# Cross-attention values carried through the output weights per head, in a transformer block with two mixture-of-experts layers

## The reference, cut to what matters

```
h1 = adaln(x);  x = mha(h1, h1, wq1, wk1, wv1, wo1) + x          # self-attention
h2 = adaln(x);  x = mha(h2, context, wq2, wk2, wv2, wo2) + x     # cross-attention
h3 = adaln(x);  x = (a * gelu(gate)) @ w2 + x                    # feed-forward

mha: q, k, v = (xq @ wq, ctx @ wk, ctx @ wv) split in 16 heads of 64
     attn = softmax(q @ k.T / sqrt(64))                          # per head, 128 x 77
     out  = concat_heads(attn @ v) @ wo + bo
```

## Time and profile before

| | |
|---|---|
| median of 3 executions | 931.8 us (930.72 to 932.12) |
| the profiled execution | 932.87 us, span 931.1 us, mean granted clock 0.917 |
| PE busy | 796.0 us, 85% |
| DVE, ACT, POOL busy | 568.6 us (61%), 540.7 us (58%), 360.9 us (39%) |
| hardware DMA queue of SP | 40027 packets, 70.09 MB, 23.5% of 16 engines |

### The profile page before, as it was taken

How to read it: one execution, slowest core, us unless ns; L and a number is a source line. 1 busy time by engine, 2 the same in 40 slices (tenths; PEclk the granted TensorE clock), 3 DMA queues, 4 the chain that set the end, 5 groups by cost and what they waited for, 6 DMA issues and landing times.

```text
span 931.1 us, 19002 instructions
## 1 busy us (share of the span) xinstructions
PE 796.0 (85%) x6173; PEld 666.3 (72%) x6173; DVE 568.6 (61%) x1941; ACT 540.7 (58%) x1147; POOL 360.9 (39%) x559
## 2 busy tenths in 40 slices
PE   5989999999999999999987688999977776861693
PEld 4767778878788888888866456999746565651693
DVE  1687778777776767766674352333458787885012
ACT  3656677666776667666764222333448898851462
POOL 1344344333433323233655150566413222226362
PEclk9999999999999999999998689999956979795797
DMA  9532033206030001000200131888500000001574
GB/s 280 198 129 107 1 129 129 106 2 231 5 120 34 19 2 37 16 23 16 65 12 19 46 105 47 241 252 246 201 18 1 1 0 1 1 1 38 164 204 125
DMA packets 43612, 78.50 MB, mean 84 GB/s; under 512 B 5564, under 2 KB 28812, under 8 KB 42876
## 3 DMA queue, kind: packets, MB, share of 16 engines
q1 hardware_dynamic: 40027, 70.09, 23.5%
q0 software_dynamic: 3488, 7.20, 2.2%
HBM read 63.98 MB, written 30.13 MB: 101 GB/s over the span
## 4 chain that ended last, share of the span: by engine, by line
PE 56%; DVE 21%; issue 8%; ACT 6%; POOL 6%; DMA 2%; DVEq 0%; SPq 0%; ACTq 0%; POOLq 0%
PE bank L635 6%; PE bank L909 5%; PE bank L697 5%; PE bank L660 4%; PE bank L650 3%; DVE sb_smax L1406 3%; PE bank L641 3%; PE bank L685 3%; PE bank L669 3%; PE bank L917 3%; DVE sb_row_sum L1416 3%; PE bank L1018 2%; DVE sb_st_all L1714 2%; PE bank L726 2%; PE bank L1026 2%
## 5 line engine op out<-in xcount | busy, mean ns | idle before, releaser
L1891 POOL TENSOR_TENSOR sb_expd<-sb_expd,sb_rden 128x512 f32<-128x512 f32 (+1 forms) x128 | 112.5, 880 | 248.3 <-DVE sb_rden L1420 248.2
L1406 DVE TENSOR_REDUCE sb_smax<-bank 128x4 f32<-128x512 f32 (+1 forms) x128 | 74.1, 579 | 59.1 <-PE bank L660 34.8
L1983 POOL TENSOR_TENSOR sb_rstd_all<-sb_rsq_all,sb_halves 128x4 f32<-128x4 f32 x44 | 45.2, 1028 | 130.7 <-DVE sb_rsq_all L1721 130.7
L685 PE MATMUL bank<-sb_eye,sb_expd 128*128 128x128 f32 (+1 forms) x512 | 77.7, 279 | 5.8 <-POOL sb_expd L1891 5.3
L1128 ACT ACTIVATE sb_expd<-sb_shifted 128x512 f32<-128x512 f32 (+1 forms) x128 | 69.8, 545 | 19.0 <-DVE sb_shifted L1409 18.0
L685 PEld LDWEIGHTS bank<-sb_eye,sb_expd 128*128 128x128 f32 (+1 forms) x512 | 60.0, 145 | 26.4 <-issue 13.2
L1122 ACT ACTIVATE sb_probT<-bank 128x512 f32<-128x512 f32 (+1 forms) x128 | 74.3, 590 | 7.2 <-PE bank L685 7.0
L1409 DVE TENSOR_TENSOR sb_shifted<-bank,sb_smax 128x512 f32<-128x512 f32 (+1 forms) x128 | 75.0, 586 | 4.4
L1416 DVE TENSOR_REDUCE sb_row_sum<-sb_expd 128x4 f32<-128x512 f32 (+1 forms) x128 | 73.0, 570 | 5.5 <-ACT sb_expd L1128 5.5
L635 PE MATMUL bank<-sb_h1T,sb_watt 128*128 128x128 f32 x512 | 71.6, 286 | 4.7 <-ACT sb_h1T L1045 2.3
L697 PE MATMUL bank<-sb_probT,sb_v 128*64 128x128 f32 (+1 forms) x1024 | 70.2, 279 | 5.0 <-issue 3.4
(11 more groups left out here) (256 smaller groups left out, 1905.7 us busy)
## 6 DMA issues: line engine op xcount, KB each, us to landing
sb_up_w<-gate_up SPq DMA_DIRECT2D x38, 384.0 KB, 4.1
rows_b<-pad_b SPq DMA_DIRECT2D x7, 1105.0 KB, 8.5
rows_a<-pad_a SPq DMA_DIRECT2D x7, 975.0 KB, 6.4
sb_up_w<-w1b SPq DMA_DIRECT2D x23, 256.0 KB, 3.5
sb_v<-v_all SPq DMA_DIRECT2D x16, 308.0 KB
v_all<-sb_v_rows SPq DMA_DIRECT2D x9, 512.0 KB, 2.6
sb_blk_x<-rows_a SPq DMA_DIRECT2D x38, 65.0 KB, 3.0
sb_watt<-att_w SPq DMA_DIRECT2D x4, 512.0 KB, 6.6
```

The costliest lines, as they stand in the source:

```text
L685: mm = pe.transpose(trans[u % 2][0:n, h, :], expd[:, (units_before(i) + u) % EXP_RING, h, 0:n], eye[:, :])
L1406: dve.tensor_reduce(smax[:, u % 2, :], s_in, X, ALU.max).then_inc(max_done, 1)
L1891: pool.tensor_tensor(e, e, rden[:, u % 2, :].unsqueeze(2).broadcast_to([P, QH, n]), ALU.mult).then_inc(norm_done, 1)
```

## The change

The cross values are now multiplied by the output weights before the attention. For each head `h`, `b2[h] = wv2[h] @ wo2[h]` is a 128 x 128 matrix; the four pieces `b2_0` to `b2_3` (four matmuls over 64 rows each) are made once, in iteration 0, and kept as 128 x 2048 in the place of the old weights. A block of values is then `context @ b2`, 2048 columns wide, in four pieces `v2_0` to `v2_3` (steps 6, 7, 9 and 10) where there were two (steps 0 and 4). `v2_all` has one row of 128 floats for each batch, head and key: 16 x 77 = 1232 rows per batch. The probabilities of a batch lie side by side as 128 x 1232 (`expd2`), are transposed in 10 chunks of 128 instead of 16 of 77 (2, 2, 3 and 3 in the four units), and the result is one accumulation of 10 matmuls at step 1 (`cross_out`, the new `wo2`). The 16 value matmuls per batch and the two `oTB` copies are gone.

`v2_rows` keeps its 128 x 1024, so it holds half a block. SP stores the first half when `v2_0` and `v2_1` are copied, the second when `v2_2` and `v2_3` are, each in one DMA for every batch that the block touches (`v2_pieces`). ACT waits with the copy of `v2_2` until the first half has landed. The load of a batch's values stands at the head of the next iteration, ahead of that iteration's stores, and needs `wo2` of two batches earlier to be over.

`v1_1` moves from step 7 to 11, `zT` from step 10 to 11, `logit` behind `v1_1`. DVE adds `wo2` to the residual ahead of the maximum of u2, where it stood behind the sum of u1. The Gelu is written over its input. The value weights' load of 512 KB moves behind that of x, transposed.

```diff
 FILL = [
-    (("h2T", "v2_0"), ("g2_5",)),
+    (("h2T",), ("g2_5",)),
     (("a2_0", "a2_1"), ("a2_2", "wo2", "rank")),
-    (("q1_1",), ("k1_0",)),
-    (("k1_1", "a2_3"), ("q1_0",)),
-    (("h3T", "v2_1"), ("g2_4",)),
-    (("g2_0", "g2_1", "g2_3"), ("gate",)),
-    (("lin",), ()),
-    (("v1_1",), ()),
+    (("q1_1", "b2_0"), ("k1_0",)),
+    (("k1_1", "a2_3"), ("q1_0", "b2_1")),
+    (("h3T", "b2_2"), ("g2_4",)),
+    (("g2_0", "g2_1", "g2_3"), ("gate", "b2_3")),
+    (("lin",), ("v2_0",)),
+    (("v2_1",), ()),
     (("wo1",), ("g2_2", "ffout")),
-    ((), ("hT",)),
-    ((), ("v1_0", "zT")),
-    (("logit",), ()),
+    (("v2_2",), ("hT",)),
+    ((), ("v1_0", "v2_3")),
+    (("zT", "v1_1"), ("logit",)),
 ]
+def v2_pieces(n):
+    found, last = [], min(P * (n + 1), B * C)
+    for b in range(P * n // C, -(-last // C)):
+        first, end = max(P * n, C * b), min(last, C * (b + 1))
+        found.append((b, first - C * b, end - C * b, first - P * n, end - P * n))
+    return found
...
             def store_values(i):
                 n = V2_BLOCK[i]
-                last = min(P, B * C - P * n)
-                sp.wait_ge(emptied["act"], max(PLAN[i, "v2_0"][2], PLAN[i, "v2_1"][2]))
-                sp.dma_start(v2_all[P * n:P * n + last, :], v2_rows[0:last, :]).then_inc(v2_stored, 16)
+                by_batch = v2_all.rearrange("(b h k) d -> b k h d", h=H, k=C)
+                for half in range(2):
+                    sp.wait_ge(emptied["act"], max(PLAN[i, f"v2_{2 * half + j}"][2] for j in range(2)))
+                    for b, k0, k1, p0, p1 in v2_pieces(n):
+                        sp.dma_start(by_batch[b, k0:k1, 8 * half:8 * half + 8, :],
+                                     v2_rows[p0:p1, :].rearrange("p (h d) -> p h d", h=8)).then_inc(v2_stored, 16)
...
             def values(i):
+                if i >= 1:
+                    load_values(i - 1)
                 if i in V2_BLOCK:
                     store_values(i)
-                load_values(i)
...
+            def cross_out(i, name):
+                t = use(i, name)
+                for c in range(CHUNKS):
+                    k = min(P, H * C - P * c)
+                    mm = pe.matmul(t[:, 0:D], probT2[0:k, c, :], v2[0:k, i % 2, c, :], start=(c == 0), stop=(c == CHUNKS - 1))
                 mm.then_inc(proj_full, 1)
...
-                    if n and name == last_of(i, "v2", first=True):
-                        act.wait_ge(v2_stored, 16 * n)
-                    empty(i, name, v2_rows[0:last, half * 512:(half + 1) * 512], lambda t: t[0:last, :])
+                    if name == "v2_0":
+                        from_one(act, v2_stored, 16 * v2_stores(n))
+                    if name == "v2_2":
+                        act.wait_ge(v2_stored, 16 * (v2_stores(n) + len(v2_pieces(n))))
+                    empty(i, name, v2_rows[0:last, half % 2 * 512:(half % 2 + 1) * 512], lambda t: t[0:last, :])
...
                 for k in range(N_STEPS):
+                    if k == AT["wo2"] and "C" in S:
+                        dve.wait_ge(xab_ready, c + 1)
+                        residual(i, "wo2", xb[:, :], tile(x0b, c))
                     if scored(k):
                         softmax_in(i, scored(k)[0], scored(k)[2])
                     if summed(k) and k != AT["sums"]:
-                        softmax_sums(i, summed(k)[0], summed(k)[2])
+                        softmax_sums(i, *summed(k))
                     if k == AT["wo2"] and "C" in S:
-                        dve.wait_ge(xab_ready, c + 1)
-                        residual(i, "wo2", xb[:, :], tile(x0b, c))
```

170 lines of the change are left out of this document (101 added, 69 removed).

## The result

The changed kernel takes 979.1 us (median of 4 runs, 977.66 to 982.12), the kernel before 931.6 in the same session: a ratio of 1.0515, 95% interval 1.0488 to 1.0541, so 47 us slower. The profiled execution is 979.36 us with a span of 977.6 and a mean granted clock of 0.895 (before 0.917).

What follows compares the result with a forecast made beforehand. PE and a chain over DVE and ACT were taken as level, within some tenths, from `gate` to `zT`. Work -5.5, wait +36 and clock +6 gave +36.5: 968 us on the median, range 945 to 984.

Steps and rivals of the forecast that it cites:

- Equal shares of rows: Stores of `v2_rows`: engine count is the largest up to 16 dividing the rows; 28 ns per 512 B run.
- The rival with shares for all engines: Stores: any row count runs on 16 engines, landing in 3.5 to 3.9 us; 930, down to 926 us; chance 0.11.
- The rival with cheap runs: Stores: equal shares, but 20 ns per run, and half the clock term; 951 us; chance 0.16.
- The third rival: PE's idle time lowers the clock everywhere, +13 for +6; 980 us with early loads or pads; chance 0.10.
- L: Landing time of the first half's stores after `v2_1`'s copy: 1.34 us plus the busiest engine's runs, 3.1 to 14.3 us.
- PE's loss to the wait: PE stops behind ACT's wait at `v2_2`, in iterations 0 and 1 at `v2_3`'s bank: +36 us, +22 at 20 ns per run.
- Clock: Granted clock falls after five new waits over 3 us, 1.2 us each: +6 us, bounds 0 and +13.
- Work: PE work removed and added over all iterations, counted by stretch with waits that go: -5.5 us, bounds -12 and +1.
- Order on DVE: Residual of `wo2` ahead of u2's maximum removes a 0.98 us wait in iteration 12 and three of 0.17.
- Idle time in iterations without v2: In iterations 5, 7, 10 and 12, PE would be idle 1.5 to 2.5 us ahead of `zT`.
- PE busy some 16 us less at full clock: PE over the whole kernel: work removed less work added, 16 us less, not itself the gain.
- The load for `b2`: Iteration 0: the 512 KB weights moved later in the queue; if late, a loss of 1 or 2 us.

Runs made afterwards that it cites:

- both halves: The changed kernel with `v2_rows` twice as wide, so ACT no longer waits for stores at `v2_2`; stores cut as before: 939.2 us, ratio 1.0051.
- PE kept busy: The changed kernel with 8, 5 and 6 needless matmuls of 512 columns ahead of `zT` in iterations 8, 11 and 13: 977.1 us, ratio 1.0467.

## Why the prediction was right, and where it was not

Forecast 968, measured 979: the mechanism, its place and its size as a sum were right, and 10 of the 11 us missed are in one term, the work.

- *Equal shares of rows, 28 ns for a run of 512 B.* The shares were right, the price of a run some 4 ns too high. First issue to landing was forecast at 14.3, 11.0, 8.5, 6.7 and 6.5 us for iterations 8, 13, 11, 0 and 3, and the traces have 12.4, 10.1, 8.9, 6.5 and 6.3; small ones came out longer (iteration 4: 5.8 for 4.1, with three DMAs). In iteration 8, at 21 GB/s, a run takes 24 ns, halfway between the 28 forecast and the 20 of the rival. The rule of the Trainium skill (DMA: Bandwidth & Descriptors, "Why a DMA increments its semaphore by 16 and not by 1") agrees: 21, 44 and about 85 GB/s for 53, 74 and 76 rows are one, two and four engines. The rival with shares for all engines falls with this, and cutting the 53 rows as 52 and 1 took the wait from 10.5 to 2.1 us. The rival with cheap runs was half right on the run and wrong on the sum: it had 25 us for wait and clock, and they cost 43. The third rival falls too: from `gate` to the next `gate` of iterations 5, 7, 10 and 12 the granted clock is 1.00 in the changed kernel, with PE's idle time in them. What L left out is that the 75 rows of iteration 8 start only when the 53 are nearly through; it came out right since the one engine's runs set the end either way.
- *PE's loss to the wait, +36 with iterations 0 and 1.* The sum is right to a few us, in part by luck. For iterations 3 to 14 I had 30.4. Against "both halves", `gate` to `zT` is longer by 2.9, 1.1, 0.3, 7.7, 0.6, 4.7 and 5.9 us in iterations 3, 4, 6, 8, 9, 11 and 13, 23.2 in all, and seven stretches behind them have a backlog of some 1.1 each: 31. Single iterations were off both ways: 8.7 for 10.6 in iteration 8, and 3.4 for 1.0 in 4 and 6 together. Iterations 0 and 1: forecast 5.5, measured 5.1 with the clock's share.
- *Clock, +6.* Near. Filling three of the five waits gave back 4.8 us, 1.6 each for 1.2 forecast, though behind the third the clock was still low for a while; with the backlog taken off, the three stretches hold some 6. But it isn't a price per microsecond of waiting: in the run with the early `v2_0`, a wait of 1.74 us cost 4.0 us behind it, backlog included.
- *Work, -5.5 with bounds of -12 and +1.* Wrong, and outside its bounds. "Both halves" is that term and stands at +4.8. Iterations 3 to 14 are near what was worked out, with 11.24 us (11.57 in iteration 12) for the 11.4 to 11.5 from `gate` to `zT` without a v2 block, and 12.3 and 12.85 for the 12.15 and 12.7 with one. Iterations 0 to 2 were to cost +2.9 (5.3 in 0, -2.4 in 1 and 2) and cost +9.8 (6.6 in 0, 3.3 in 1). Of that, 1.4 is `b2`: its pieces take 1.09 us each, 4.4 and not 3.0. The row that I used is of three pieces of `a2` back to back; a single one between other work took 1.09 us already before the change:

```profile
30.16 1.16 PE L719 MATMUL bank<-sb_g 64*128 64x128 f32 x8
31.25 0.66 PE L685 MATMUL bank<-sb_eye,sb_expd 128*128 128x128 f32 x4
```

  Most of the rest I put down to an error of method: I summed PE's work for two iterations in which DVE does nearly as much (22.7 us of 29.5 in iteration 1, PE 25.1), and didn't ask how long DVE would wait for the next scores behind three more pieces. That wait went from 0.35 to 3.12 us. This is read from traces and not shown: no run took `v2_3` or `v1_1` away from there, and the clock's second fall in iteration 1 was never filled.
- *Order on DVE, -1.8 in iteration 12 and a little elsewhere.* The wait went, and the total didn't move (ratio 1.0004). With both halves iteration 12, from `zT` to `zT`, is 1.3 us shorter than before.
- *Idle time in iterations without v2, 1.5 to 2.5 us ahead of `zT`.* The size was right (1.84), the place half: 0.96 ahead of `zT`, 0.88 ahead of u7's transposes.
- *PE busy some 16 us less at full clock.* The page has 798.2 us for 796.0. The lower clock stretches that number, so it shows neither way; with both halves it is 790.1.
- *The load for `b2`, 1 or 2 us if late.* Left out of the sum, and it came 0 to 2.64 us late in the profiles, 0.28 in the first of the changed kernel.

## What to carry to other kernels

Read the shape of a DMA as well as its bytes: a store of 212 KB cut at an odd row took 12 us, one of 512 KB in 128 rows 2.6. The packets under 512 B tell how many engines took part (16 for 128 rows, 11 for 77, one and fifteen for 53 and 75). A buffer halved to save space turns such a landing into a wait in an engine's queue, and everything behind it pays; look for every later use of that buffer, too, and not just for the one that the change is about. And a sum of one engine's work holds only where the others have slack, which at a pipeline's start they may not have.

## What else the runs showed

- A store behind one that sits on a single engine can be slow to issue: the pairs of 53 and 75 rows held SP for 8.43 and 8.40 us in iteration 8, and 8.42 and 8.43 in the run with early `v2_0`; with the 53 rows cut, three stores took 1.56. That a full queue of the one engine held SP is my reading, no row names it. No wait of another engine is put down to this.
- The level of the clock behind the same wait isn't the same in every execution. `zT` to `gate` behind iteration 4 was 17.9 in two executions of the changed kernel and 19.5 in two kernels whose edits all lie behind it (the 53 rows cut, PE kept busy), with a clock of 1.00 and 0.83 over the first 10 us; that alone moves a total by 1 to 2 us.
- The phases behind the first block took 402.5 us in one session and 417.4 in another with the same kernel; what makes the difference stays open.
